# Routing of a two-layer expert network: one-hot slots built from f16 halves with the token tile innermost, the lane column on ScalarE, one scan for all experts

## The reference

```
# layer 0: E = 4 experts, K = 2 choices
probs = softmax(xf @ router_w + router_b)
top_p, top_i = top_k(probs, 2)
top_p = top_p / sum(top_p)                      # gates
out = sum over the two choices of top_p * expert[top_i](x)     # silu(x w1) * (x w3), then w2
# layer 1: E = 8 experts, one choice
route = sigmoid(x @ Wr + br)
out = max(route) * expert[argmax(route)](x)     # gelu(x W1), then W2
```

## Time and profile before

| what | value |
|---|---|
| runs of the kernel | 2027.1, 2024.3, 2026.25 us; median 2026.25 |
| profiled execution | 2028.43 us, span of its instructions 2026.7 us |
| mean granted TensorE clock | 0.885 of full speed |
| TensorE busy | 1671.5 us (82%) |
| VectorE busy | 1183.9 us (58%) |
| GpSimd busy | 1091.8 us (54%) |
| ScalarE busy | 853.8 us (42%) |
| DMA | 164.96 MB, mean 81 GB/s |

### The profile page before, as it was taken

One profiled execution on the slowest core, in us unless ns is written; L12 is line 12 of the kernel. 1 busy time (PEld: TensorE's weight loads), 2 busy tenths in 40 slices (PEclk: granted clock), 3 DMA queues, 4 the chain that ended last, 5 costly groups with the idle time before them and its releaser, 6 DMA issues.

```text
span 2026.7 us, 32145 instructions
## 1 busy us (share of the span) xinstructions
PE 1671.5 (82%) x11048; PEld 1002.3 (49%) x11048; DVE 1183.9 (58%) x1908; ACT 853.8 (42%) x1897; POOL 1091.8 (54%) x905
## 2 busy tenths in 40 slices
PE   6699989973699999999999468777776574899992
PEld 3355555542466666666666233322331253577771
DVE  6789988977323323322332687999899687122224
ACT  3444444342244444444444375443442263344443
POOL 3377777623333333333342699999999663233322
PEclk8699999975799999999999679888886586899996
DMA  5013333017122232222232410000000374111115
...
DMA packets 109287, 164.96 MB, mean 81 GB/s; under 512 B 27457, under 2 KB 74065, under 8 KB 109009
## 3 DMA queue, kind: packets, MB, share of 16 engines
...
## 4 chain that ended last, share of the span: by engine, by line
PE 61%; DVE 14%; POOL 13%; issue 5%; DMA 3%; ACT 3%; SPq 0%; POOLq 0%; DVEq 0%; ACTq 0%
PE ps L555 53%; POOL BIG L1828 11%; DVE BIG L1014 7%; PE ps L815 5%; ACT BIG L1512 2%; DVE X L1014 1%; PE ps L787 1%; DMA BIG<-YT 1%; DVE bnst L1023 1%; POOL X L1828 1%; PE ps L730 1%; POOL BIG L1942 1%; DVE BIG L1456 1%; DVE BIG L1434 1%; PE ps L670 1%
## 5 line engine op out<-in xcount | busy, mean ns | idle before, releaser
L555 PE MATMUL ps<-BIG 128*128 (+8 forms) x8100 | 1315.7, 341 | 197.1 <-POOL BIG L1828 70.7
L555 PEld LDWEIGHTS ps<-BIG 128*128 128x128 f16 (+2 forms) x8100 | 737.0, 104 | 708.9 <-issue 142.3
L1828 POOL TENSOR_TENSOR BIG<-BIG 128x256 f16<-128x256 f32 (+4 forms) x553 | 779.0, 1435 | 254.0 <-ACT BIG L1512 240.8
L1512 ACT ACTIVATE BIG<-ps 128x512 f16<-128x512 f16 (+5 forms) x1008 | 395.3, 445 | 590.3 <-PE ps L555 261.2
L1014 DVE TENSOR_TENSOR BIG<-ps,BIG 128x512 f32<-128x512 f32 (+3 forms) x725 | 476.9, 711 | 284.5 <-ACT BIG L1512 227.2
L1915 POOL DMA_INDIRECT YT<-BIG x106 | 105.2, 992 | 548.6 <-ACT BIG L1512 548.6
L1014 DVE TENSOR_TENSOR BIG<-BIG,ps 128x512 f32<-128x512 f32 (+1 forms) x202 | 120.4, 600 | 419.2 <-PE ps L555 403.4
L1512 ACT ACTIVATE BIG<-BIG 128x256 f16<-128x256 f32 (+2 forms) x354 | 208.6, 606 | 137.3 <-DVE BIG L1014 98.3
L1655 ACT ACTIVATE BIG<-ps 128x512 f32<-128x512 f32 x212 | 127.0, 599 | 138.2 <-PE ps L555 138.2
L1456 DVE TENSOR_REDUCE BIG<-BIG 128x160 f32<-128x2560 f32 x64 | 185.2, 2894 | 0.0
L1911 POOL DMA_INDIRECT BIG<-HB,BIG x106 | 103.3, 974 | 35.0 <-issue 26.3
...
## 6 DMA issues: line engine op xcount, KB each, us to landing
...
HB<-BIG SPq DMA_DIRECT2D x64, 128.0 KB, 3.4
X<-in_x SPq DMA_DIRECT2D x4, 1024.0 KB, 12.1
```

The lines of the kernel that those rows point to most:

```text
L555: return e.matmul(o, lhsT, rhs, start=start, stop=stop, skip_group_check=True)
L1512: return e.activation(o, i, ACT.Copy)
L1828: return e.tensor_tensor(o, a, b, op)
```

## The change

- Layer 0's softmax is no longer divided by its sum. The gates are computed behind the loop of step 5 instead of ahead of `AL`.
- `ct` comes out of TensorE with experts outermost (its operand is read in that order). One scan over all E x 32 counts, reading PSUM, multiplies the running sum by `first`, which is 0 at each expert's first tile. `cs` and the clearing of `zz` on VectorE go.
- Slots of both choices are computed together in `WS` and `SLs`; so is the split into `s_hi` and `s_lo`, which are f16 now.
- A unit's tables are laid out with the token tile innermost: `A0` and `A1` as [NS, 8], `S1` as [128, 8]. VectorE compares with the f16 tables `tile8` and `lane8`, of the same shape, and multiplies by `tok` (128 x tile number plus 128), for `A1[:, 0]`. ScalarE makes `A1[:, 1]` from `A0` with a per-partition scale. GpSimd has no part in it. TensorE reads column r of the tables with a step of 8 elements.
- `cmp` to `ei` move behind the loop. `pad` moves behind `gi`.
- GpSimd builds `first`, `zz`, `lane8`, `tile8` and `tok` ahead of the loop; `iota_p` and `tile_no` at the kernel's start go.
- GpSimd's first gather waits for `gi`; only `put` waits for `yi`.

```diff
-                self.SL = [area(NT) for _ in range(CH)]
+                self.SLs = area(CH, NT)
...
-                self.OH = [area(NT, E) for _ in range(CH)]
-                self.dec = area(E)
-                self.CI, self.zz, self.cs = area(E, NT), area(NT), area(E, NT)
+                self.OHs, self.WS = area(CH, NT, E), area(CH, NT, E)
+                self.OH = [self.OHs[:, c] for c in range(CH)]
+                self.dec, self.first = area(E), area(E, NT)
+                self.CI, self.zz = area(E, NT), area(E)
...
-                self.it, self.ex, self.it128 = area(NS), area(NS), area(NS)
+                self.ex, self.it128 = area(NS), area(NS)
+
+                self.lane8, self.tile8 = area(128, 8, dt=f16), area(NS, 8, dt=f16)
+                self.tok = area(CH, NT, dt=f16)
...
-                self.s_i, self.s_lo, self.s_hi, self.s_j = area(NT).bitcast(i32), area(NT), area(NT), area(NT).bitcast(i32)
-                self.S1 = over.ring(3, 8, 128, dt=f16)
-                self.A1 = over.ring(3, 8, 2, NS, dt=f16)
+                self.s_i, self.s_j = (area(CH * NT).bitcast(i32).rearrange("p (c t) -> p c t", c=CH) for _ in range(2))
+                self.s_lo, self.s_hi = area(CH, NT, dt=f16), area(CH, NT, dt=f16)
+                self.A0 = area.ring(2, NS, 8, dt=f16)
+                self.S1 = over.ring(3, 128, 8, dt=f16)
+                self.A1 = over.ring(3, 2, NS, 8, dt=f16)
...
-                self.rk, self.ct = bank(1, NT, E), bank(2, NT, E)
+                self.rk, self.ct = bank(1, NT, E), bank(2, E, NT)
...
                 mm(m_.rk, stri[:, :], m_.AL, True, True)
-                mm(m_.ct, ones[:, :], m_.AL, True, True).then_inc(s["rt_ps"], 1)
+                mm(m_.ct, ones[:, :], m_.AL.rearrange("p t e -> p e t"), True, True).then_inc(s["rt_ps"], 1)
                 for c in range(m_.CH):
                     for g in range(4):
                         n = 4 * c + g
                         pe.wait_ge(s["rt"], rt_at[l, "S1", n])
-                        pe.wait_ge(s["a1_p"], at(l, "a1_p") + n + 1)
+                        pe.wait_ge(s["a1_a"], at(l, "a1_a") + n + 1)
                         for r in range(8):
-                            m = mm(m_.mp, m_.S1[n % 3][:, r, :], m_.A1[n % 3][:, r, :, :], n == 0 and r == 0,
+                            m = mm(m_.mp, m_.S1[n % 3][:, :, r], m_.A1[n % 3][:, :, :, r], n == 0 and r == 0,
                                    n == 4 * m_.CH - 1 and r == 7)
                         m.then_inc(s["mp_ps"], 1)
...
-                    n = c.next()
-                    e.tensor_reduce(MX, PR, AX.X, ALU.add).then_inc(n, 1)
-                    n = c.next()
-                    e.reciprocal(MX, MX).then_inc(n, 1)
-                    n = c.next()
-                    tt(PR, PR, bc(MX, 2, E), ALU.mult).then_inc(n, 1)
                 else:
                     rt_at[l, "PR"] = c.n
                     dve.wait_ge(s["rt_a"], 2)
...
-                    dve.wait_ge(s["it"], at(l, "it") + 3)
+                    dve.wait_ge(s["it"], at(l, "it") + 8)
                     tt(W3, W3, bc(m_.dec, 1, NT), ALU.mult).then_inc(n, 1)
...
+                n = c.next()
+                if CH == 2:
+                    tt(m_.AL, OH[0], OH[1], ALU.add).then_inc(n, 1)
+                else:
+                    e.tensor_copy(m_.AL, OH[0]).then_inc(n, 1)
+                rt_at[l, "AL"] = c.n
+
+                ct = m_.ct
+                dve.wait_ge(s["rt_ps"], l + 1)
+                n = c.next()
+                e.tensor_tensor_scan(out=m_.CI.rearrange(FLAT), data0=m_.first.rearrange(FLAT), data1=ct.rearrange(FLAT), initial=0.0,
+                                     op0=ALU.mult, op1=ALU.add).then_inc(n, 1)
...
+                n = c.next()
+                tt(m_.CI, m_.CI, ct, ALU.subtract).then_inc(n, 1)
+                n = c.next()
+                tt(m_.CI, m_.CI, bc(m_.bases, 2, NT), ALU.add).then_inc(n, 1)
+                n = c.next()
+                tt(m_.PS, m_.rk, m_.CI.rearrange("p e t -> p t e"), ALU.add).then_inc(n, 1)
+                n = c.next()
+                tt(m_.WS, bc(m_.PS, 1, CH), m_.OHs, ALU.mult).then_inc(n, 1)
+                n = c.next()
+                e.tensor_reduce(m_.SLs, m_.WS, AX.X, ALU.add).then_inc(n, 1)
+                n = c.next()
+                e.tensor_copy(m_.s_i, m_.SLs).then_inc(n, 1)
+                n = c.next()
+                e.tensor_scalar(m_.s_j, m_.s_i, 7, None, ALU.arith_shift_right).then_inc(n, 1)
+                n = c.next()
+                e.tensor_copy(m_.s_hi, m_.s_j).then_inc(n, 1)
+                n = c.next()
+                e.scalar_tensor_tensor(out=m_.s_lo, in0=m_.s_hi, scalar=-128.0, in1=m_.SLs, op0=ALU.mult, op1=ALU.add).then_inc(n, 1)
+                at_s = c.n
...
+                for u in range(4 * CH):
+                    ch, g = u // 4, 8 * (u % 4)
+                    s1, a1, hot = m_.S1[u % 3], m_.A1[u % 3], m_.A0[u % 2]
+                    if u >= 3:
+                        dve.wait_ge(s["mp_ps"], at(l, "mp_ps") + u - 2)
+                    if u >= 2:
+                        dve.wait_ge(s["a1_a"], at(l, "a1_a") + u - 1)
+                    dve.wait_ge(s["rt"], at_s)
+                    tt(hot, bc(m_.s_hi[:, ch, g:g + 8], 1, NS), m_.tile8, ALU.is_equal).then_inc(s["rt"], 1)
+                    tt(s1, bc(m_.s_lo[:, ch, g:g + 8], 1, 128), m_.lane8, ALU.is_equal).then_inc(s["rt"], 1)
+                    rt_at[l, "A1", u] = c.n + 1
+                    dve.wait_ge(s["rt"], rt_at[l, "A1", u])
+                    tt(a1[:, 0], hot, bc(m_.tok[:, ch, g:g + 8], 1, NS), ALU.mult).then_inc(s["rt"], 1)
+                    c.n += 3
+                    rt_at[l, "S1", u] = c.n
                 if CH == 2:
                     n = c.next()
                     tt(MX, GV[0], GV[1], ALU.add).then_inc(n, 1)
...
-                    n = c.next()
-                    tt(m_.AL, OH[0], OH[1], ALU.add).then_inc(n, 1)
-                else:
-                    n = c.next()
-                    e.tensor_copy(m_.AL, OH[0]).then_inc(n, 1)
-                rt_at[l, "AL"] = c.n
-                n = c.next()
-                e.memset(m_.zz, 0.0).then_inc(n, 1)
-                dve.wait_ge(s["rt_ps"], l + 1)
-                n = c.next()
-                e.tensor_copy(m_.cs, m_.ct.rearrange("p t e -> p e t")).then_inc(n, 1)
-                for x in range(E):
-                    n = c.next()
-                    e.tensor_tensor_scan(out=m_.CI[:, x, :], data0=m_.cs[:, x, :], data1=m_.zz, initial=0.0, op0=ALU.add, op1=ALU.add).then_inc(n, 1)
...
-                for ch in range(CH):
-                    n = c.next()
-                    tt(W3, m_.PS, OH[ch], ALU.mult).then_inc(n, 1)
-                    n = c.next()
-                    e.tensor_reduce(SL[ch], W3, AX.X, ALU.add).then_inc(n, 1)
...
-                for ch in range(CH):
-                    n = c.next()
-                    e.tensor_copy(m_.s_i, SL[ch]).then_inc(n, 1)
-                    n = c.next()
-                    e.tensor_scalar(m_.s_j, m_.s_i, 7, None, ALU.arith_shift_right).then_inc(n, 1)
-                    n = c.next()
-                    e.tensor_copy(m_.s_hi, m_.s_j).then_inc(n, 1)
-                    n = c.next()
-                    e.scalar_tensor_tensor(out=m_.s_lo, in0=m_.s_hi, scalar=-128.0, in1=SL[ch], op0=ALU.mult, op1=ALU.add).then_inc(n, 1)
-                    for g4 in range(4):
-                        g, u = 8 * g4, 4 * ch + g4
-                        s1, a1 = m_.S1[u % 3], m_.A1[u % 3]
-                        if u >= 3:
-                            dve.wait_ge(s["mp_ps"], at(l, "mp_ps") + u - 2)
-                        n = c.next()
-                        tt(a1[:, :, 0, :], bc(m_.s_hi[:, g:g + 8], 2, NS), bc(m_.it, 1, 8), ALU.is_equal).then_inc(n, 1)
-                        n = c.next()
-                        e.tensor_scalar(a1[:, :, 1, :], a1[:, :, 0, :], pcol[:, 0:1], None, ALU.mult).then_inc(n, 1)
-                        rt_at[l, "A1", u] = c.n
-                        n = c.next()
-                        tt(s1, bc(m_.s_lo[:, g:g + 8], 2, 128), bc(iota_p[:, :], 1, 8), ALU.is_equal).then_inc(n, 1)
-                        rt_at[l, "S1", u] = c.n
                 dve.wait_ge(s["mp_ps"], at(l, "mp_ps") + 4 * CH)
                 n = c.next()
-                e.tensor_scalar(m_.pad, m_.mp[:, 0, :], 1.0, None, ALU.is_lt).then_inc(n, 1)
-                n = c.next()
-                e.tensor_scalar(m_.rf, m_.mp[:, 0, :], 128.0, -128.0, ALU.mult, ALU.add).then_inc(n, 1)
+                e.tensor_scalar(m_.rf, m_.mp[:, 0, :], -128.0, None, ALU.add).then_inc(n, 1)
                 n = c.next()
...
                 rt_at[l, "gi"] = c.n
+                n = c.next()
+                e.tensor_scalar(m_.pad, m_.mp[:, 0, :], 1.0, None, ALU.is_lt).then_inc(n, 1)
                 dve.wait_ge(s["rt_p"], l + 1)
...
+                for u in range(4 * m_.CH):
+                    act.wait_ge(s["rt"], rt_at[l, "A1", u])
```

(60 more changed lines are left out.)

5 lines of the change are left out of this document (1 added, 4 removed).

## The result

The changed kernel takes 2002.72 us (median of 4 runs, 2000.47 to 2007.54), the kernel before 2026.67 us (4 runs, 2024.3 to 2027.41): a ratio of 0.9887, 95% interval 0.9867 to 0.9907. The forecast was 2000.0 us in a range of 1996 to 2012; the gain is 24 us where 26.3 were forecast. The two routing stages together became 25.85 us shorter.

A forecast was written before the change was run, and what follows sets the result against it. The prediction took VectorE's serial chain through both layers' routing as the bound. Savings of 18.2 us in layer 0 and 8.1 in layer 1, 26.3 together, gave 2000.0 us against the median 2026.25, range 1996 to 2012.

The forecast's parts named there:

- The front of layer 0: Layer 0's routing ahead of the one-hot loop: softmax, gates, scan, slot sums, `cmp` to `ei`, second conversion; 6.36 us shorter.
- The compares' rate: VectorE's f16 compares in the loop: 0.52 ns an element, 0.44 us for 536 and 0.70 us for 1024 elements.
- A unit of three operations: VectorE's compare hi, compare lo and multiply in the one-hot loop: 1.69 us in layer 0, 1.45 us in layer 1.
- I take it as hidden: TensorE's strided reads in the loop cost nothing: 1.69 us a unit for what took 1.05, deciding only from 1.6 times.
- the second rival: TensorE's strided reads bound the loop; at 2.5 times today's matmul time 9.2 us lost, 2009 us; chance 0.13.
- My own sign of being wrong: In the loop, VectorE idling for TensorE or ScalarE, compares staying at 0.7 and 1.2 us, or VectorE waiting for GpSimd's tables.
- The tail counts: VectorE's steps moved behind the loop count on the chain: 2.47 us in layer 0, 1.47 us in layer 1.
- After the loop's result: Between loop and gather, five VectorE steps leave the chain: 1.25 us saved in layer 0, 1.1 in layer 1.
- The gather: Layer 0's first gather, 4.12 us, now issued ahead of SP's weight loads: 0.6 us saved, range 0 to 1.27.
- GpSimd's tables: GpSimd builds the new tables before the loop in some 2.5 us, ready at 474.5, needed at 475.6: hidden.
- ScalarE's lane column: ScalarE's step in each loop unit, after compare hi: 630 ns, hidden beside 1.2 us of VectorE's other two steps.
- The slower rival: TensorE's strided reads slow the loop by 3.8 times, costing 26.3 us, so the kernel is slower than before; chance 0.03.

The follow-up runs named there:

- one_rate: step8 with the two comparison tables and the slot halves in f32 instead of f16: 2005.06 us (one run; before 2029.27).
- step8: The changed kernel with four token tiles innermost instead of eight, so TensorE reads at 8 bytes instead of 16: 1993.73 us, ratio 0.9834.
- gather_yi: step8 with GpSimd waiting for `yi` ahead of its first gather, as before the change: 1995.69 us (one run; before 2029.27).
- bulk_later: step8 with SP holding its layer 1 weight loads until the first gather has been transposed: 1993.16 us (one run; before 2026.92).
- weights_dense: The changed kernel with only `S1` back in dense order, so VectorE's 1024-element compare writes at a step: 2042.03 us (one run; before 2027.17).

## Why the prediction was right, and where it was not

- **The front of layer 0** (softmax, gates, scan, slot sums, `cmp`, second conversion): forecast 6.36 us less, measured 15.02 - 10.36 + 1.71 = 6.37 (15.02 from the stage's start to the first compare). The single scan takes 0.42 us (forecast 0.43), layer 1's 0.69 (0.70); the subtraction that now reads PSUM 0.29, nothing extra.
- **The compares' rate**: right, and by the half of the f16 tensor-scalar's rate that it was taken from; one_rate shows the alternative.
- **A unit of three operations**: the sum was mis-sized. I put 0.035 us of gap between operations; that holds where each waits for the one before. In the new loop none is held by the one just ahead of it (the product waits for compare hi, two back), each starts some 0.08 us before the one ahead ends, and the three, 0.43 + 0.69 + 0.43 = 1.55 us by their durations, take 1.30 from unit to unit (layer 1: 1.07, forecast 1.45). Forecast error: 8 x 0.39 + 4 x 0.38 = 4.6 us too slow.
- **"I take it as hidden"** is the step that failed. TensorE went to 1.97 us a unit, 1.88 times, over the 1.6 I had named as the limit, and above all over the 1.24 that hold against a unit of 1.30. Its cost is 17.25 - 13.06 = 4.2 us in layer 0 and 6.11 - 5.93 = 0.2 in layer 1. I had a row (1.64 times) and the rule, and costed them at 0.3 us; the second rival's mechanism is what happened, at k = 1.88 instead of 2.5. The row was misread, too: 705 and 1157 ns are means of single, overlapping matmuls, not rates. In this change such means rose only 1.35 times (313 to 423 ns) where the busy time rose 1.88 times, so neither the row's 1.64 nor its 6% by busy time gave the price. My own sign of being wrong, VectorE idle in the loop for TensorE, is in the timeline (0.28 to 0.57 us from the fifth unit on). The two errors nearly cancel, and that is luck: layer 0's loop and tail are 16.0 - 3.1 + 4.2 = 17.1 (measured 17.25), layer 1's 7.3 - 1.5 + 0.2 = 6.0 (6.11). With the unit priced right and TensorE still taken as hidden, the forecast would have been 4.6 us lower.
- **The tail counts**: it doesn't in the changed kernel (TensorE's last 1.98 us of wait cover it), and does in step8.
- **After the loop's result**: 3.23 to 1.87 us, 1.36 saved (1.25 forecast), and 2.91 to 1.69, 1.22 (1.1). gather_yi gives 1.24 and 1.17 of it back.
- **The gather**: 4.12 to 4.02 us, 0.1 saved where I took 0.6 from a range of 0 to 1.27. The bulk loads' price is real (bulk_later: 1.3 us), but the order of issue doesn't avoid it.
- **GpSimd's tables**: hidden, but for some 0.07 us, and with no slack left. An iota of 1024 elements in rows of eight takes 1932 ns, 1.9 ns an element where I took 0.7 from a dense one. The tables end at 477.80 us, and VectorE's operation that needs them starts at 477.91, 0.1 us after the one before it, where the usual gap is 0.035; in step8 the four iotas take 2.15 us instead of 3.26.
- **ScalarE's lane column**: 743 ns, hidden, as forecast.
- **The slower rival** needed k = 3.8; it falls with the measured 1.88. It would have come by another way: with an array written at a step instead of read at one, as in weights_dense, the kernel is slower than before (2042.03 against 2027.17 us, one run; its layer 0 stage 62.5 against 51.84).

Summed: layer 0 saves 6.37 + 8.74 (25.99 - 17.25, where 10.0 were forecast) + 1.36 + 0.10 = 16.57 us (18.2 forecast), layer 1 9.29 (8.1; its loop 11.06 - 6.11 = 4.95 where 3.8 were forecast), together 25.9 against 26.3. The medians' 24 us fit within what the stretches outside differ by.
